# Top-32 cross-attention: the list rounds of two tiles interleaved, and everything behind the lists one step later

## The reference

```python
Q = split_heads(x @ Wq.T + bq)                     # 16 heads of 8
K = split_heads(knowledge @ Wk.T + bk)             # 1601 keys
V = split_heads(knowledge @ Wv.T + bv)
scores = einsum('bhsd,bhnd->bhsn', Q, K) / sqrt(8)
topk_scores, topk_indices = top_k(scores, 32)
weights = softmax(topk_scores)
out = (sum over the 32 chosen keys of weights * V) @ Wo.T + bo
```

## Time and profile before

| what | value |
|---|---|
| time, median of 3 runs | 4364.22 us (4359.03 to 4367.62) |
| the profiled execution | 4360.38 us |
| its span, first to last instruction | 4358.7 us |
| busy over the whole span | PE 80%, DVE 78%, ACT 65%, POOL 23% |
| tile loop of this stage | from about 2672 to 4142 us of the span |

### The profile page before, as it was taken

How to read it: one execution, slowest core, us unless ns; L and a number is a source line. 1 busy time by engine, 2 the same in 40 slices (tenths; PEclk the granted TensorE clock), 3 DMA queues, 4 the chain that set the end, 5 groups by cost and what they waited for, 6 DMA issues and landing times. The chain is left out here.

```text
span 4358.7 us, 70735 instructions
## 1 busy us (share of the span) xinstructions
PE 3495.7 (80%) x25855; PEld 2827.9 (65%) x25855; DVE 3400.7 (78%) x5326; ACT 2819.5 (65%) x4654; POOL 1014.7 (23%) x929
## 2 busy tenths in 40 slices
PE   6445749999999788999999885777777777777788
PEld 3334337999999566999999852555555555555576
DVE  4675877777777624877787656999999999999844
ACT  3112616666666444666666534999999999999832
POOL 0000503111210201211121011434444343443310
PEclk9555869999999889999999987999999999999998
DMA  8743011111110121111110001000000000000000
GB/s 275 107 61 106 4 41 39 39 31 39 39 31 16 24 64 36 39 31 31 39 39 24 22 7 41 16 16 16 31 16 16 16 16 31 16 16 9 1 23 19
DMA packets 186341, 161.29 MB, mean 37 GB/s; under 512 B 7996, under 2 KB 174092, under 8 KB 185996
## 3 DMA queue, kind: packets, MB, share of 16 engines
q1 hardware_dynamic: 182604, 142.83, 12.4%
q10 hardware_dynamic: 3392, 13.93, 0.9%
HBM read 127.36 MB, written 20.20 MB: 34 GB/s over the span
## 5 line engine op out<-in xcount | busy, mean ns | idle before, releaser
L559 PEld LDWEIGHTS psU<-ctxN,ST 128*128 128x128 f32 x6656 | 853.7, 191 | 98.5 <-issue 39.8
L559 PE MATMUL psU<-ctxN,ST 128*128 128x129 f32 x6656 | 868.1, 275 | 20.8 <-issue 20.8
L1169 DVE MAX8 top<-pairs 128x8 f32<-128x801 f32 (+1 forms) x512 | 709.2, 1406 | 8.9
L1134 POOL TENSOR_TENSOR P<-P,EX 128x1601 f32<-128x1601 f32 x128 | 459.6, 3591 | 711.2 <-ACT P L1049 711.2
L645 ACT ACTIVATE ST<-ST 128x512 f32<-128x512 f32 (+1 forms) x832 | 513.1, 625 | 167.2 <-DVE ST L747 163.2
L944 PE MATMUL psU<-ctxN,PT 128*128 128x129 f32 (+1 forms) x3328 | 439.7, 285 | 173.8 <-ACT PT L1057 173.8
L747 DVE TENSOR_TENSOR ST<-ST,psB 128x512 f32<-128x512 f32 (+1 forms) x832 | 556.3, 677 | 3.2 <-PE psB L578 3.2
L733 DVE TENSOR_TENSOR psA<-psA,ST 128x512 f32<-128x512 f32 x640 | 446.6, 698 | 137.2 <-ACT ST L637 69.4
L944 PEld LDWEIGHTS psU<-ctxN,PT 128*128 128x128 f32 (+1 forms) x3328 | 404.2, 197 | 196.8 <-ACT PT L1057 196.6
L1174 DVE MATCH_REPLACE8 pairs<-top,pairs 128x801 f32<-128x801 f32 (+1 forms) x384 | 482.2, 1256 | 0.0
L547 PE MATMUL psS<-statL,ctxH 128*128 128x512 f32 x832 | 393.6, 473 | 5.6 <-ACT ST L637 2.7
(11 more groups left out here) (505 smaller groups left out, 6194.6 us busy)
## 6 DMA issues: line engine op xcount, KB each, us to landing
ctxN<-in_ctx SPq DMA_DIRECT2D x48, 768.0 KB
ahead_ctxT<-ctxT_scratch SPq DMA_DIRECT2D x32, 800.5 KB, 4.3
ctxT_scratch<-trn ACTq DMA_DIRECT2D x16, 800.5 KB
ctxT<-ctxT_scratch SPq DMA_DIRECT2D x16, 800.5 KB, 6.1
nat<-in_ctx SPq DMA_DIRECT2D x16, 768.0 KB
dist_scratch<-dd SPq DMA_DIRECT2D x8, 800.5 KB
skewed<-in_ctx SPq DMA_DIRECT2D x8, 768.0 KB
ctx_late<-in_ctx SPq DMA_DIRECT2D x8, 768.0 KB
```

Source lines behind the costliest of these rows:

```text
L559: last = pe.matmul(psU[:, q, 0:D + 1], ST[0:n, i % SLOTS, q * 128:q * 128 + 128], ctxN[0:n, j, k, 0:D + 1], start=(k == 0 and q % 2 == 0), ...
L1134: pool.tensor_tensor(P[:, j, :], P[:, j, :], EX[:, j, :], ALU.mult).then_inc(p_ready, 1)
L1169: dve.max(top[:, j, 8 * n:8 * n + 8], pairs[:, j, 0:width]).then_inc(listed, 1)
```

## The change

DVE's step s now holds six list instructions of tile s and of tile s-1 in turn: find 0 of tile s, find 2 of tile s-1, drop 0 of s, drop 2 of s-1, find 1 of s, inverse(s-4), find 3 of s-1, drop 1 of s, an addition, and both folds of tile s+1. The two semaphores `listed_early` (rounds 0 and 1) and `listed_late` (rounds 2 and 3) take the place of `listed`. `top` has three buffers for two. All that stands behind the lists moves one step back against copy_scores and scores: count_sides(s-2), norm(s-4), copy_weights(s-3), mark(s-2), negate(s-1), exps(s-1), copy_ut(s-4) on ACT, and turn, turn_u, values, sums on PE. `keyed` moves one tile forward, so the keys are made in the same steps as before. The loops have T + 3 steps. No arithmetic is added or removed. The diff, with context cut:

```diff
--- before.py
+++ after.py
...
     TOPK = 32
-    LISTS = 7
+    EARLY, LATE = 4, 3
     PARTS = 4
...
         PT = c.sb(st, "PT", [128, 2, NC, 128])
-        top = c.sb(st, "top", [128, 2, TOPK])
+        top = c.sb(st, "top", [128, 3, TOPK])
         mneg = c.sb(st, "mneg", [128, 2])
...
         BLOCKS = len(KB)
-        keyed = {TB * b + 1 + n: (b + 1, n) for b in range(B - 1) for n in range(BLOCKS)}
+        keyed = {TB * b + n: (b + 1, n) for b in range(B - 1) for n in range(BLOCKS)}
         uses = []
...
         scored, copied = c.sem("scored"), c.sem("copied")
-        folded, listed, max_ready = c.sem("folded"), c.sem("listed"), c.sem("max_ready")
+        folded, max_ready = c.sem("folded"), c.sem("max_ready")
+        listed_early, listed_late = c.sem("listed_early"), c.sem("listed_late")
         exp_done, marked = c.sem("exp_done"), c.sem("marked")
...
                 scores(0)
-                for s in range(T + 2):
+                for s in range(T + 3):
                     if s + 1 < T:
                         scores(s + 1)
-                    t = s - 2
+                    t = s - 3
                     if t in summed:
...
                 def negate(t):
-                    act.wait_ge(listed, LISTS * t + 1 + ONE)
+                    act.wait_ge(listed_early, EARLY * t + 1 + ONE)
                     if t >= 2:
                         act.wait_ge(exp_done, t - 1 + ONE)
-                    act.activation(mneg[:, t % 2:t % 2 + 1], top[:, t % 2, 0:1], ACT.Copy, scale=-1.0
+                    act.activation(mneg[:, t % 2:t % 2 + 1], top[:, t % 3, 0:1], ACT.Copy, scale=-1.0
                                    ).then_inc(max_ready, 1)
...
                 def exps(t):
...
                 def count_sides(t):
                     j = t % 2
-                    edge = top[:, j, TOPK - 1:TOPK]
-                    act.wait_ge(listed, LISTS * (t + 1) + ONE)
+                    edge = top[:, t % 3, TOPK - 1:TOPK]
+                    act.wait_ge(listed_early, EARLY * (t + 1) + ONE)
+                    act.wait_ge(listed_late, LATE * (t + 1) + ONE)
                     if t:
...
                         act.wait_ge(counted, t + ONE)
-                    act.activation(listed_sides[:], top[:, j, :], ACT.Sign, scale=-1.0, bias=edge,
+                    act.activation(listed_sides[:], top[:, t % 3, :], ACT.Sign, scale=-1.0, bias=edge,
                                    accum_out=above[:, j:j + 1]).then_inc(counted, 1)
...
                 def mark(t):
...
                 copy_scores(0)
-                for s in range(T + 2):
-                    if 0 <= s - 1 < T:
-                        count_sides(s - 1)
+                for s in range(T + 3):
+                    if 0 <= s - 2 < T:
+                        count_sides(s - 2)
                     if s + 1 < T:
                         copy_scores(s + 1)
+                    if s >= 4:
+                        norm(s - 4)
+                    if s - 3 in keyed:
+                        keys(*keyed[s - 3])
                     if s >= 3:
-                        norm(s - 3)
-                    if s - 2 in keyed:
-                        keys(*keyed[s - 2])
-                    if s >= 2:
-                        copy_weights(s - 2, 0)
-                        copy_weights(s - 2, 1)
+                        copy_weights(s - 3, 0)
+                        copy_weights(s - 3, 1)
+                    if 0 <= s - 2 < T:
+                        mark(s - 2)
+                    if s >= 3:
+                        copy_weights(s - 3, 2)
+                        copy_weights(s - 3, 3)
                     if 0 <= s - 1 < T:
-                        mark(s - 1)
-                    if s >= 2:
-                        copy_weights(s - 2, 2)
-                        copy_weights(s - 2, 3)
-                    if s < T:
-                        negate(s)
-                        exps(s)
-                    if s >= 3:
-                        copy_ut(s - 3)
+                        negate(s - 1)
+                        exps(s - 1)
+                    if s >= 4:
+                        copy_ut(s - 4)
                 norm(T - 1)
...
                     if t >= 2:
-                        dve.wait_ge(listed, LISTS * (t - 1) + ONE)
+                        dve.wait_ge(listed_late, LATE * (t - 1) + ONE)
                     if low:
...
 
-                def find(t, n, width):
-                    j = t % 2
+                def find(t, n):
+                    pairs_t, top_t = pairs[:, t % 2], top[:, t % 3]
                     if n == 0:
                         dve.wait_ge(folded, 2 * t + 1 + ONE)
-                        if t >= 2:
-                            dve.wait_ge(sided, t - 1 + ONE)
-                            dve.wait_ge(counted, t - 1 + ONE)
-                            dve.wait_ge(max_ready, t - 1 + ONE)
+                        if t >= 3:
+                            dve.wait_ge(sided, t - 2 + ONE)
+                            dve.wait_ge(counted, t - 2 + ONE)
+                            dve.wait_ge(max_ready, t - 2 + ONE)
+                    elif n == 1:
+                        dve.wait_ge(listed_early, EARLY * t + 2 + ONE)
+                    elif n == 2:
+                        dve.wait_ge(folded, 2 * t + 2 + ONE)
+                        dve.wait_ge(listed_early, EARLY * t + 4 + ONE)
                     else:
-                        dve.wait_ge(listed, LISTS * t + 2 * n + ONE)
-                    if n == 2:
-                        dve.wait_ge(folded, 2 * t + 2 + ONE)
-                    dve.max(top[:, j, 8 * n:8 * n + 8], pairs[:, j, 0:width]).then_inc(listed, 1)
-
-                def drop(t, n, width):
-                    j = t % 2
-                    dve.wait_ge(listed, LISTS * t + 2 * n + 1 + ONE)
-                    dve.match_replace(pairs[:, j, 0:width], top[:, j, 8 * n:8 * n + 8], pairs[:, j, 0:width], LOW
-                                      ).then_inc(listed, 1)
+                        dve.wait_ge(listed_late, LATE * t + 2 + ONE)
+                    dve.max(top_t[:, 8 * n:8 * n + 8], pairs_t[:, 0:HALF if n < 2 else KP]
+                            ).then_inc(listed_early if n < 2 else listed_late, 1)
+
+                def drop(t, n):
+                    pairs_t, top_t = pairs[:, t % 2], top[:, t % 3]
+                    own = pairs_t[:, 0:HALF if n < 2 else KP]
+                    if n < 2:
+                        dve.wait_ge(listed_early, EARLY * t + 2 * n + 1 + ONE)
+                    else:
+                        dve.wait_ge(listed_late, LATE * t + 1 + ONE)
+                    dve.match_replace(own, top_t[:, 8 * n:8 * n + 8], own, LOW
+                                      ).then_inc(listed_early if n < 2 else listed_late, 1)
 
                 def inverse(t):
...
                 fold(0, True)
-                for s in range(T + 2):
-                    if s < T:
-                        find(s, 0, HALF)
-                        drop(s, 0, HALF)
-                        find(s, 1, HALF)
-                    if s >= 3:
-                        inverse(s - 3)
-                    if s < T:
-                        drop(s, 1, HALF)
-                    if s < T:
-                        find(s, 2, KP)
-                    if s - 2 in summed:
-                        add(*summed[s - 2])
+                for s in range(T + 3):
+                    early, late = s < T, 0 <= s - 1 < T
+                    if early:
+                        find(s, 0)
+                    if late:
+                        find(s - 1, 2)
+                    if early:
+                        drop(s, 0)
+                    if late:
+                        drop(s - 1, 2)
+                    if early:
+                        find(s, 1)
+                    if s >= 4:
+                        inverse(s - 4)
+                    if late:
+                        find(s - 1, 3)
+                    if early:
+                        drop(s, 1)
+                    if s - 3 in summed:
+                        add(*summed[s - 3])
                     if s + 1 < T:
                         fold(s + 1, False)
-                    if s < T:
-                        drop(s, 2, KP)
-                    if s + 1 < T:
                         fold(s + 1, True)
-                    if s < T:
-                        find(s, 3, KP)
                 inverse(T - 1)
...
```

## The result

The changed kernel takes 4342.2 us (median of 4 runs, 4336.3 to 4344.3) against 4365.9 before (4359.0 to 4368.9): a ratio of 0.9942, 95% interval 0.9928 to 0.9956, 19 to 31 us less. The forecast was 4349, its range 4337 to 4361 and its own part of that 4344 to 4353: the result lies in the range, 2 us under the forecast's own part.

A forecast was written before the change was run, and what follows sets the result against it. The prediction took DVE as the bound and ACT's ring over PE as the next, 11.15 us per tile: 25 us gained up to copy_scores(127) less 10 at the end gives 15, so 4349 against the median; range 4337 to 4361.

The forecast's parts named there:

- The junctions: DVE's three find/drop neighbours that wait for each other: interleaving saves 0.10 and twice 0.11, step 11.29 to 10.97 us.
- The rule on the junctions: Trainium skill on DVE: a semaphore after each of eight copies costs nothing; by it DVE's term would be 0.
- Rival 2: The junctions give nothing: DVE stays at 11.29 per tile and the extra end step is paid, 4372 us; chance 0.06.
- ACT's ring as the new bound: Last copy_weights, PE's values and scores, copy_scores: 11.67, 11.29 or 10.72 us per tile, 89.2 per batch.
- DVE's waits: DVE's fold (L1155) waits for ACT's copy (L1009) some 15 us in all, in tiles with keys.
- Rival 3: ACT's ring shortens, so DVE's 88.1 us per batch counts: gain 30, 4334 us; chance 0.06.
- The middle: From copy_scores(4) to copy_scores(127): 1369.9 us, plus 1 for disturbances; copy_scores(127) starts 25 earlier.
- Additions and the clock: PE's turn_u waits for DVE's later addition: 0 more taken, bounds 0 and 0.7 us in each of 7 pairs.
- Rival 1: ACT's ring bounds but PE's clock falls in addition tiles (5 us), end costs 2 more: 4357 us; chance 0.15.
- The start: Up to copy_scores(4), which was to start at 2707.8 instead of 2710.63.
- The end: From copy_scores(127) to count_sides(127), where the extra step is paid: 29.5 us instead of 19.6.
- what I put on top for PE's slow clock: At the end, PE idles more: 0 to 2 us on top, 1.5 taken.

The follow-up runs named there:

- experiment 5: Drops 0 and 2 put right behind their finds, in a scores-early kernel without ACT's listed-sign sum (4353.4 us) and in the changed kernel (4345.8 us).
- experiment 2: Changed kernel with DVE's list rounds of a tile in a row again, extra step kept: 4386.0 us; with find 2's two waits swapped back, 4372.4.
- Experiment 3: Changed kernel without ACT's activation that sums the signs of the listed scores (-31 instead): 4343.2 us.
- experiments 4 and 6: PE's scores(s+2) before the last quarter of values (4), or between groups 1 and 2 (6); against the changed kernel: 4333.5 and 4335.8 us, variants 4335.7, 4316.4, 4308.8.
- e9: Changed kernel with PE's scores(s+2) between groups 1 and 2 of values(s-3): 4335.8 us.
- e4b: Changed kernel with PE's scores(s+2) before the last quarter of values(s-3), not scores(s+1) at the next step's head: 4333.5 us.
- experiment 4: Changed kernel with PE's scores(s+2) before the last quarter of values(s-3): 4333.5 us; also without ACT's sum of the listed scores' signs: 4335.7 us.
- e7b: Experiment 4's second kernel (scores early, no listed-sign sum) with drops 0 and 2 right behind their finds: 4353.4 us.

## Why the prediction was right, point by point

- **The junctions.** Right that they cost DVE time, low in size. Forecast 10.97 per step, measured 10.83: a junction is worth 0.11 to 0.14, not 0.10 to 0.11, and the reciprocal takes 0.06, not 0.12. The last was a fourth junction that I did not count. In the earlier trace rows the load of drop 1 (3413.32) starts 0.04 after find 1, whose result it needs, has ended; the reciprocal between them did not cover that wait. As DVE is not the bound, all this gave next to nothing.
- **The rule on the junctions.** The Trainium skill, VectorE: DVE Perf Modes, The DRAIN you can't avoid, says that a semaphore after each of eight copies cost nothing. The runs disagree with it for the list instructions: 0.27 us per tile for two junctions in experiment 5, 31.1 us of stage for the interleaving in experiment 2. Rival 2 fell with it.
- **ACT's ring as the new bound.** Right: 11.67, 11.29 and 10.71, and the wait of 0.22 or 0.23 in 122 tiles of 128. Experiment 3 shows that it closes over PE and is not ACT's load; experiments 4 and 6 that DVE bounds next once it is open. DVE's waits were 26 us for the 15 forecast (without the one at the start), as its step was 0.14 shorter. Rival 3 fell.
- **The middle.** 1369.0 us for 1369.9 forecast. My 1 us for disturbances on top did not come. By my count DVE's step stood only 1.1 us per batch under the ring, so which of the two bounds was a close call. Experiment 5 shows how little hung on it: with DVE's step at 11.10 the middle took 3.1 more.
- **Additions and the clock.** Right for the changed kernel: PE's longest wait for an addition is 0.9, for 2.2 and 3.0 before, and the tiles with additions keep 10.72. One of the three of 16 tiles:

```profile
3137.48 0.30 PE L957 MATMUL psZ<-ident,U 128*128 128x128 f32 x1 [0.61 <-DVE x L1198]
```

  Rival 1 did not happen here, but it is what ate e9. In e4b some tiles took 12.3 to 13.3 behind such a wait too, but DVE's waits for the values behind a lowered clock are 2 us there, and those in tiles with keys the rest.
- **The start** gave 3.4 for 2.8 forecast.
- **The end** was the term sized worst: 7.7 lost in front of count_sides(127) for 9.9, and the rest ran 0.9 faster. Of the 2.2, 1.5 is what I put on top for PE's slow clock: it was at 0.50 from C + 10 to C + 14, yet the only wait of ACT between C and count_sides(127) is norm(123)'s for its reciprocal. The other 0.7 is that wait, which ended at C + 11.2 for 11.9.

Together 21.0 of stage for 15. The medians say 23.7, and their interval (19 to 31) holds the 21 and not the 15; the forecast was right in sign and mechanism and some 6 us low.

## What to carry to other kernels

When a saturated engine is relieved, read from the trace the tiles in which the next engine was not held up: as long as that engine keeps its neighbours, their period is the new time. Here it gave 1369.9 for a measured 1369.0. Interleaving two tiles' chains removed the neighbours' waits, and the extra step of pipeline depth cost 8 to 10 us at the end. Before an engine's work is cut, look where it stands: work right in front of a wait for another engine only lengthens that wait (experiment 3), and there the order helps. And when an order has been changed, read again which engine waits for nothing: in experiment 4 the bound had already moved from the ring to DVE, and the periods of ACT did not tell.

## What the runs showed of the hardware that I had not expected

- Which of two waits comes last before an instruction counts: with the list's semaphore last, drop 1 to find 2 took 1.16 us, with the fold's last 1.09, and 9.5 us of stage hung on it.
- A MAX8 of 801 columns is left after 0.90 when another tile's instruction follows, and in e7b after 1.03 when its own drop does; in the kernel before it was 1.01.
- In the kernel before, four of PE's six waits of 2.2 us for an addition were followed by the 1.2 GHz level, and in e9 all seven of 3.3 us, where the clock fell before the wait was over; of the waits of 0.6 to 0.9 in the changed kernel none was. An addition placed 0.9 us earlier in DVE's order decided 17 us of stage.
